# Grouped attention: four turns of a head pair in one block, value products in two, scores in two blocks of two

## The reference

```python
def _L1_xattn_ref(query, key, value, mask, Wq, Wk, Wv, Wo):   # batches of 128 tokens
    q = (query @ Wq).reshape(b, t, 32, 128)
    k = (key @ Wk).reshape(b, t, 8, 128)
    v = (value @ Wv).reshape(b, t, 8, 128)
    q, k = apply_rope(q), apply_rope(k)
    logits = einsum('btkgd,bTkd->bkgtT', q.reshape(b, t, 8, 4, 128), k) * 0.0883883
    logits = 30.0 * tanh(logits / 30.0)
    logits = where(mask, logits, -1e+30)
    weights = softmax(logits, axis=-1)
    attn = einsum('bkgtT,bTkd->btkgd', weights, v).reshape(b, t, 32 * 128)
    return attn @ Wo

x = x + _L1_xattn_ref(_layernorm(x), ctx_4096, ctx_4096, mask, Wq, Wk, Wv, Wo)
```

## Time and profile before

| | |
|---|---|
| median of 3 runs | 1614.78 us (1614.23 to 1615.20) |
| the profiled execution | 1615.26 us |
| its span, first to last instruction | 1613.5 us |
| mean granted PE clock | 0.998 of full speed |
| PE busy | 1598.8 us, 99% |
| DVE, ACT, POOL busy | 999.5, 748.1 and 878.4 us |

### The profile page before, as it was taken

How to read it: one execution, slowest core, us unless ns; L and a number is a source line. 1 busy time by engine, 2 the same in 40 slices (tenths; PEclk the granted TensorE clock), 3 DMA queues, 4 the chain that set the end, 5 groups by cost and what they waited for, 6 DMA issues and landing times.

```text
span 1613.5 us, 25021 instructions
## 1 busy us (share of the span) xinstructions
PE 1598.8 (99%) x8512; PEld 1365.9 (85%) x8512; DVE 999.5 (62%) x1528; ACT 748.1 (46%) x1922; POOL 878.4 (54%) x688
## 2 busy tenths in 40 slices
PE   9989999999999999999999999999999999999999
PEld 7878888888888888888888887888898898889887
DVE  7523333636666676676679677776656656665675
ACT  5331111225454544554553334656645546654653
POOL 6344444537466575565569775544536435443445
PEclk9999999999999999999999999999999999999999
DMA  9434444513333332333341211101100111010011
GB/s 345 172 125 157 153 151 153 180 40 130 108 120 106 107 123 94 107 123 94 114 150 47 59 41 50 60 33 33 53 34 27 47 40 33 27 47 20 21 53 53
DMA packets 52111, 146.44 MB, mean 91 GB/s; under 512 B 7264, under 2 KB 12000, under 8 KB 51520
## 3 DMA queue, kind: packets, MB, share of 16 engines
q1 hardware_dynamic: 52032, 145.41, 26.0%
HBM read 107.64 MB, written 37.75 MB: 90 GB/s over the span
## 4 chain that ended last, share of the span: by engine, by line
PE 94%; DVE 2%; POOL 1%; ACT 1%; issue 1%; DMA 0%; SPq 0%; ACTq 0%; DVEq 0%; POOLq 0%
PE banks L55 27%; PE banks L57 26%; PE banks L56 26%; PE banks L2283 4%; PE banks L783 3%; PE banks L803 3%; PE banks L792 2%; PE banks L2290 2%; PE banks L224 1%; ACT resid L993 0%; DMA rawA<-in_x_wK 0%; DVE resid L1933 0%; POOL wtA_lo L1428 0%; ACT x_probs L1055 0%; DMA g_swapped<-in_l_b 0%
## 5 line engine op out<-in xcount | busy, mean ns | idle before, releaser
L2747 POOL TENSOR_TENSOR g_swapped<-g_swapped,rawB 128x512 f32<-128x512 f32 x80 | 103.0, 1290 | 171.2 <-ACT g_swapped L2429 171.2
L1526 POOL TENSOR_TENSOR x_probs<-x_probs,x_inv 128x512 f32<-128x512 f32 x64 | 66.6, 1040 | 170.9 <-DVE x_inv L1317 168.0
L1055 ACT ACTIVATE x_probs<-x_probs,x_top 128x128 f32<-128x128 f32 x256 | 99.5, 390 | 92.2 <-DVE x_top L1308 92.2
L1428 POOL TENSOR_TENSOR wtA_lo<-rawA,wtA_hi 128x1024 fp32r<-128x1024 f32 (+1 forms) x31 | 72.1, 2326 | 100.2 <-ACT wtB_hi L964 78.8
L1193 DVE COPY c_v_kept<-banks 128x512 f32<-128x512 f32 x64 | 44.1, 690 | 108.1 <-PE banks L57 108.1
L2577 DVE TENSOR_TENSOR g_turned_by<-banks,rawB 128x512 f32<-128x512 f32 x80 | 55.2, 690 | 85.8 <-ACT g_swapped L2429 85.8
L2741 POOL TENSOR_TENSOR g_probs<-g_probs,g_inv 128x512 f32<-128x512 f32 x64 | 67.7, 1079 | 74.5 <-DVE g_inv L2568 74.4
L55 PE MATMUL banks<-wtV_hi,g_att_lo 128*128 128x512 f32 x256 | 104.3, 407 | 0.0
L55 PE MATMUL banks<-xT_hi,wtO_lo 128*128 128x512 f32 x256 | 102.9, 402 | 0.0
L2428 ACT COPY g_swapped<-banks 64x512 f32<-64x512 f32 x80 | 46.7, 583 | 120.3 <-PE banks L57 113.6
L56 PE MATMUL banks<-wtV_lo,g_att_hi 128*128 128x512 f32 x256 | 100.3, 392 | 0.0
(11 more groups left out here) (353 smaller groups left out, 5155.2 us busy)
## 6 DMA issues: line engine op xcount, KB each, us to landing
kept_k<-c_k_kept SPq DMA_DIRECT2D x16, 1024.0 KB, 4.0
x_k<-kept_k SPq DMA_DIRECT2D x32, 512.0 KB, 4.5
kept_v<-c_v_kept SPq DMA_DIRECT2D x14, 1024.0 KB, 4.9
x_v<-kept_v SPq DMA_DIRECT2D x28, 512.0 KB, 3.5
rawA<-in_x_wQ SPq DMA_DIRECT2D x16, 512.0 KB, 4.4
rawO<-in_x_wO SPq DMA_DIRECT2D x16, 512.0 KB, 3.5
rawO<-in_g_wQ SPq DMA_DIRECT2D x16, 512.0 KB, 3.5
rawV<-in_g_wO SPq DMA_DIRECT2D x16, 512.0 KB, 3.5
```

Source lines behind the costliest of these rows:

```text
L1055: e = nc.scalar.activation(probs[:, b, :], probs[:, b, :], ACT.Exp, bias=top[:, b:b + 1], accum_out=total[:, b:b + 1])
L1428: return pool.tensor_tensor(wt[into][1][:, cut], raw[kind][:, cut], f32(wt[into][0][:, cut]), ALU.subtract)
L1526: pool.tensor_tensor(probs[:, part, :], probs[:, part, :], rows, ALU.mult).then_inc(probs_ready, 1)
L2747: pool.tensor_tensor(part, part, sin[:, :].unsqueeze(1).to_broadcast([P, HB, P]), ALU.mult)\
```

## The change

It moves instructions on PE alone, in `body`: all four turns of pair p - 1 stand in one block behind query block 1; value products 0 and 1 stand together, and so do 2 and 3; the scores come two quarters at a time, 0 and 1 behind output batch 0, 2 and 3 behind output batch 2. Nothing is added or left out, and the waits are inside the moved steps. The three other engines and the transfers keep their order. The first pair's front half (`start`) and the last pair's back half behind the loop stay as they were.

```diff
                 query(r, u, 0)
                 query(r, u, 1)
-                turn(p - 1, 0)
-                turn(p - 1, 1)
+                for j in range(4):
+                    turn(p - 1, j)
                 query(r, u, 2)
...
                 pv(p - 1, 0, before_kv)
-                turn(p - 1, 2)
                 pv(p - 1, 1, before_kv)
-                turn(p - 1, 3)
                 if not second:
                     query(r, u, 3)
                 weights_ready("O", p - 1)
                 pv(p - 1, 2, before_kv)
+                pv(p - 1, 3, before_kv)
                 output_batch(r, u, 0)
                 scores(p, 0, rope_of(r, u, 1, 0))
-                pv(p - 1, 3, before_kv)
+                scores(p, 1, rope_of(r, u, 1, 0))
                 output_batch(r, u, 1)
-                for j in range(1, 4):
-                    scores(p, j, rope_of(r, u, 1, j // 2))
-                    if j < 3:
-                        output_batch(r, u, j + 1)
-                for b in range(4, B):
+                output_batch(r, u, 2)
+                scores(p, 2, rope_of(r, u, 1, 1))
+                scores(p, 3, rope_of(r, u, 1, 1))
+                for b in range(3, B):
                     output_batch(r, u, b)
```

## The result

The changed kernel takes 1631.91 us (median of 4 runs, 1630.35 to 1632.69) against 1614.62 us (median of 4, 1614.23 to 1615.20). The ratio is 1.0106, with a 95% interval of 1.0091 to 1.0121: 17.3 us slower, inside the predicted range and 2.5 us above the predicted 1629.4. The profiled execution took 1631.94 us, with a span of 1630.1 us.

What follows compares the result with a forecast made beforehand. PE's own instruction stream, plus waits opening in it, was taken as the bound. 14 x 1.06 + 1.0 - 1.2 = 14.6 us on the profiled 1615.26 gives 1629.9, less 0.48 for the median: 1629.4; range 1625 to 1632.5.

Steps and rivals of the forecast that it cites:

- The chain: From query block 2's end over ACT, POOL and DVE; DVE's low parts start 3.98 and 5.17 us behind value product 0.
- The two hand-over times: From DVE's start to PE's start, read at two places where PE waited: 0.83 and 0.74 us; 0.74 was taken.
- the room of product 2: Before the change, value product 2 could start at 1261.84 and started at 1262.18: 0.34 us to spare.
- the two waits: PE idle before value products 2 and 3 in fourteen bodies, 0.58 then 0.48 us, together 1.06 us late.
- The waits that were costed at nothing: Later scores of quarters 0 and 1, and turns 2 and 3 asking for probabilities 3.5 and 4.2 us earlier: no cost.
- the waits being hidden: Rival: PE's stream has slack the trace does not show, or the change acts otherwise on PE; 1613.6 us, chance 0.05.
- the second wait: Rival: later scores delay the softmax, next body's turns wait half a microsecond in each of 15; 1637 us, chance 0.03.
- the dear edges: Rival: each block edge on PE costs 0.09 us, four fewer give 0.35 us a body; 1625.4 us, chance 0.08.
- grouping: Seven blocks of 128-column instructions become three per body on PE: gain 0.08 us a body, 1.2 us over fifteen.
- (e): First body, query block 3 ahead of value product 0: existing 0.85 us wait before value product 2 grows; 1.0 us counted.
- The rule on the clock: Skill page: transposes don't count as busy for PE's clock like other matmuls, so the clock might fall in each body.
- the clock falls: Rival: 1.2 GHz behind each block of sixteen turns, 3.3 us, 15 times; about 1679 us, chance 0.01.

## Why the prediction was right

**The mechanism**, point by point. The chain's length from value product 0, 3.98 and 5.17 us, was forecast to stay and measured 3.99 and 5.19. The two hand-over times, 0.83 and 0.74, turned out to be both right, the first for product 2 and the second for product 3; I had taken the second for both. So the room of product 2 before was 0.25 us and not 0.34, and the two waits were 0.64 and 0.39 us and not 0.58 and 0.48; their sum, 1.03, hangs on product 3 alone and came out right within 0.03. Product 2's first matmul carries three waits in the program's order and product 3's one, which may be the difference; no run changed it. The waits are where they were said to be, in fourteen bodies and the first, and moving the one step that holds the chain on POOL takes them away in the fourteen. The waits that were costed at nothing cost nothing: the table of PE's waits has none before turns or output batches, and the one before scores, 0.5 us ahead of the loop, is there in the kernel before too. In the shortest round trip DVE is busy for 20.38 us (20.02 before) and ACT for 18.64 (18.28), so little changed there. Of the rivals, the waits being hidden, the second wait and the dear edges fall with the traces.

**The sizes.** In the fourteen bodies I had 1.06 us of lateness less 0.08 of grouping, 0.98 each or 13.7 us together; the round trips grew by 14.8. The experiment with DVE's step moved gives the reference without waits, and splits it for the body shown:

| term, us a body | predicted | measured |
|---|---|---|
| product 3 later than due | 1.06 | 1.03 (+5.92 against +4.89) |
| lost behind the wait | 0 | 0.09 (1271.01 to 1273.21 is 2.20, against 1264.65 to 1266.76, 2.11) |
| grouping | -0.08 | -0.04 (30.12 to 30.08), -0.07 with a key block only |

The middle term is one that I did not have. The first matmul of product 3 behind its wait is followed after 0.22 us and not 0.12 (1271.01 to 1271.23); of product 2 it is 0.19 (1269.91 to 1270.10), which costs nothing more, since product 3 then waits anyway. The trace of before held it: in the tail, where PE had waited, the same pair stands 0.22 apart (1571.31 to 1571.53), and I used that place for the start of the first alone. Why the pair is spaced so was not tested.

**The first body** was put at 1.0 us and cost 2.47. The step that failed is (e): what I counted there, the lengthened wait, is about 0.9 of it; the other 1.5 us are the output products and value product 3 at the lower clock. From value product 3 to the scores is 3.74 us (1054.50 to 1058.24) where it is 2.20 in the other bodies. That the waits came so near to 1.0 was partly luck: the terms named in (e), 0.87 for the turns and 1.20 less 0.71 for product 3, make 1.36 and not 1.0. Measured, the wait before product 2 grew by 0.52 us, since DVE's low part came sooner behind value product 0 (2.14 us in place of 2.49), and product 3 added some 0.4; the first round trips of the kernels with the turns alone and with the value products alone, 0.51 and 0.40 us longer than before, say the same. The median's 2.5 us over the forecast is made of these 1.5 us and of the 1.1 us (14.8 less 13.7) in the fourteen others.

**The rule on the clock.** The rival "the clock falls" was worked out for each block of sixteen turns, and that is refuted: the granted clock was 1.00 over a round trip that holds one, and in the kernel with the old first body the fourteen blocks left the upper level alone. The Trainium skill, page "TensorE: Matmul & The Clock Gate", section "Part 4: PE-mode transpose", says that transposes don't count as busy for the clock in the way other matmuls do; no run here shows an effect of it, with 1.7 us of them in a body. Where the clock did fall, PE had stood idle 1.37 us and 0.16 us, with value product 2 between, and the block of turns lay nearly 10 us back (it ends at 1044.89). It fell there in the profile of the changed kernel and in that with DVE's step moved, which have both waits. It did not fall in the profile of the kernel with the turns alone, which has a wait of 1.38 us but not the second one, nor in those with value products alone (0.84 and 0.16 us) and with three turns ahead (0.94 and 0.16 us), which have the second one behind a shorter first. With one profile of each kernel this is a pattern and not a shown cause. The spread of the kernel with DVE's step moved, seven times from 1614.70 to 1615.10 us and four times from 1616.30 to 1617.63, is of the size of one such stretch, and may be that; but the work ahead of the first body, the same in all ten profiles, took from 1042.93 to 1044.79 us too. Why one execution falls and another doesn't was not settled.

**What it was for.** Grouping 128-column instructions was worth 0.04 to 0.07 us a body, some 0.8 us of 1615. The scores alone gave nothing that could be measured. Seen against that, the order that the change gave up brought the operand of value product 2 with 0.25 us to spare and that of product 3 with 2.06, and the change took all of it.

## What to carry to other kernels

- Where PE is busy without a gap, work moved forward past a step pushes back everything that hangs on that step, and work moved away from between two hand-overs is cover lost. Both are read from the timeline before the edit: the distance from a producer's start to its consumer's, less the hand-over time at a place where the consumer did wait. Count 0.1 us more for the last restart of a group.
- If PE's order is to change, look for the step on another engine that is in the chain only by its written order. Here one sum of 0.6 us stood ahead of four steps that did not need it, and dragged a product on POOL into the chain; moving it bought back all of the waits in the fourteen bodies.
- A wait can cost more than its length: here, in two of the profiles, two waits of 1.5 us together were followed by a low clock that cost another 1.5. Sum the loss with and without it.

## What the runs showed of the hardware

- The granted clock halved behind idle times of 1.37 and 0.16 us, 1.1 us apart, in a stream that was otherwise without a gap, and stayed at 0.50 for some 3.4 us; the same stream kept 1.00 with one idle time of 0.85 us, and in one profile with one of 1.38. In the idle time of 4.20 us the lower level came some 2.9 us behind its start (100.69 to about 103.6).
- A PE that restarted from a wait lost 0.07 us (value product 2) or 0.1 us (product 3) in the spacing of its first two matmuls, the latter where the wait is shown as only 0.15 us long.
- Sixteen transposes in one block run at the pitch of eight. From the start of the block to value product 0 it is 4.48 us (1260.61 to 1265.09) with sixteen and 3.64 (1253.48 to 1257.12) with eight: eight more for 0.84 us, with the clock at 1.00.
